# Sorting expert rows by one-hot products on TensorE in place of a trip through DRAM

## What is computed

```python
def _bank_residual(x2, Wr, br, W1, b1, W2, b2):     # twice: bank sp, bank fq
    logits = x2 @ Wr + br
    probs = softmax(logits); expert = argmax(probs); gate = probs[expert]
    oneh = one_hot(expert, 8)
    pos = (cumsum(oneh, axis=0) * oneh).sum(-1) - 1          # place within its expert
    slot = expert * CAP + pos                                # CAP is never reached here
    buf = zeros(...).at[slot].add(x2)                        # rows sorted by expert
    h = gelu(einsum('ecd,edf->ecf', buf, W1) + b1)           # 512 -> 128
    out = einsum('ecf,efd->ecd', h, W2) + b2                 # 128 -> 512
    return out.reshape(...)[slot] * gate                     # back to node order
# x = x + bank_sp + bank_fq + gelu(x2 @ Ws1 + bs1) @ Ws2 + bs2
```

## Time and profile before

| | us |
|---|---|
| median of 3 runs (522.31 to 524.74) | 523.99 |
| the profiled execution | 524.64 |
| its span, first to last instruction | 522.6 |
| TensorE busy in it | 468.2 (90%) |
| VectorE, ScalarE, GpSimd busy | 226.3, 180.3, 199.7 |

### The profile page before, as it was taken

One profiled execution on the slowest core, in us unless ns is written; L12 is line 12 of the kernel. 1 busy time (PEld: TensorE's weight loads), 2 busy tenths in 40 slices (PEclk: granted clock), 3 DMA queues, 4 the chain that ended last, 5 costly groups with the idle time before them and its releaser, 6 DMA issues.

```text
span 522.6 us, 7439 instructions
## 1 busy us (share of the span) xinstructions
PE 468.2 (90%) x2586; PEld 336.7 (64%) x2586; DVE 226.3 (43%) x559; ACT 180.3 (35%) x388; POOL 199.7 (38%) x217
## 2 busy tenths in 40 slices
PE   2788999989999997989999999999999999999930
PEld 2444547777665654766577777777777787887720
DVE  4879961313442727532220023320037665565542
ACT  2799672222211114511150033230265434333210
POOL 3103000191500802692507806142054847943422
PEclk9999899989999999999999999999999999999875
DMA  5999999968999789768207100304042532534665
GB/s 125 410 425 419 424 411 362 327 242 274 418 409 424 238 291 422 299 229 266 97 1 229 52 0 1 105 0 126 1 101 61 153 90 81 186 120 147 191 228 179
DMA packets 39636, 111.88 MB, mean 214 GB/s; under 512 B 6711, under 2 KB 12966, under 8 KB 31150
## 3 DMA queue, kind: packets, MB, share of 16 engines
q1 hardware_dynamic: 36558, 108.16, 56.8%
q0 software_dynamic: 3040, 3.22, 2.4%
HBM read 97.37 MB, written 13.98 MB: 213 GB/s over the span
## 4 chain that ended last, share of the span: by engine, by line
PE 74%; DMA 9%; issue 7%; POOL 3%; ACT 2%; SPq 2%; DVE 1%; POOLq 0%; DVEq 0%
PE ps L1457 16%; PE ps L1459 15%; PE ps L1458 15%; PE ps L1816 9%; PE ps L1481 8%; DMA ring<-in_L_gnn_basis_dram 8%; PE ps L1542 2%; POOL got L716 2%; PE ps L1661 2%; DMA got<-y_dram,slot_u 1%; ACT h_tmp L1217 1%; PE ps L1465 1%; POOL piece_lo L643 1%; PE ps L1719 1%; POOL piece_hi L642 1%
## 5 line engine op out<-in xcount | busy, mean ns | idle before, releaser
L1481 PE MATMUL ps<-ring,sel_att 128*32 128x512 f32 x512 | 66.1, 602 | 6.9 <-DMA ring<-in_L_gnn_basis_dram 3.4
L1457 PE MATMUL ps<-piece_hi,ht_hi 128*125 128x512 f32 x140 | 56.1, 401 | 0.8 <-PE ps L1459 0.6
L642 POOL CAST piece_hi<-piece_raw 128x512 fp32r<-128x512 f32 x28 | 19.8, 708 | 94.4 <-issue 69.9
L970 DVE SCALAR_TENSOR_TENSOR u_lo<-ps,gates,u_hi 125x512 fp32r<-125x512 f32 x20 | 15.0, 751 | 94.1 <-ACT u_hi L1365 94.1
L1458 PE MATMUL ps<-piece_lo,ht_hi 128*125 128x512 f32 x140 | 55.1, 394 | 0.0
L1459 PE MATMUL ps<-piece_hi,ht_lo 128*125 128x512 f32 x140 | 55.1, 394 | 0.0
L699 POOL TENSOR_TENSOR w_lo<-unit_raw,w_hi 128x512 fp32r<-128x512 f32 x32 | 40.5, 1291 | 33.2 <-ACT w_hi L1347 33.1
L643 POOL TENSOR_TENSOR piece_lo<-piece_raw,piece_hi 128x512 fp32r<-128x512 f32 x28 | 37.8, 1349 | 13.2 <-issue 11.1
L820 DVE TENSOR_SCALAR oh_n<-iota_n,keys 125x626 f16<-125x626 f16 x100 | 38.3, 383 | 8.0 <-PE ps L1542 5.9
L1816 PE MATMUL ps<-u_hi,cf 125*125 125x512 f32 x100 | 39.9, 399 | 1.3 <-PE ps L1459 1.3
L1816 PE MATMUL ps<-u_lo,cf 125*125 125x512 f32 x100 | 39.4, 394 | 0.0
(11 more groups left out here) (321 smaller groups left out, 982.7 us busy)
## 6 DMA issues: line engine op xcount, KB each, us to landing
ring<-in_L_gnn_basis_dram SPq DMA_DIRECT2D x64, 1024.0 KB, 9.3
y_dram<-ybuf SPq DMA_DIRECT2D x24, 256.0 KB, 2.0
rel_dram<-stag SPq DMA_DIRECT2D x16, 256.0 KB, 8.3
w_raw<-rel_dram SPq DMA_DIRECT2D x8, 512.0 KB, 7.0
unit_raw<-in_L_ffn_W_sp_dram SPq DMA_DIRECT2D x16, 256.0 KB, 3.0
unit_raw<-in_L_ffn_W_fq_dram SPq DMA_DIRECT2D x16, 256.0 KB, 2.8
piece_raw<-in_L_mix_Wkqv_dram SPq DMA_DIRECT2D x3, 1024.0 KB, 9.8
piece_raw<-in_L_mix_W_dram SPq DMA_DIRECT2D x2, 1024.0 KB, 10.2
```

The lines of the kernel that those rows point to most:

```text
L642: own_step(pool.tensor_copy(hi, raw))
L970: dve.scalar_tensor_tensor(out=u_lo[l][:, t, :], in0=ps[0:TP, u_bank(i), :], scalar=gates[:, t, r:r + 1], in1=u_hi[l][:, t, :].bitcast(F32 ...
L1457: pe.matmul(target, a_hi, b_hi, start=first, stop=False, skip_group_check=skip)
L1481: last = pe.matmul(ps[32 * c:32 * c + 32, rel_bank(ch), :], sel_att[:, ch // CHUNKS, g].rearrange("p r q -> p (r q)"), ring[slot][:, c * D ...
```

## The change

Slots come in blocks of 32 (`SB`): `NB` is 27 blocks a bank, 864 slots, taken four to a tile of up to 128 slots (`NY` = 7 tiles a bank, the last of three blocks). The way through DRAM (`scatter`, `read_back`, `turn_block_rows`, the zeroing) is gone. Instead GpSimd builds for each node tile a one-hot matrix of 125 rows x 864 slots (`sort_tile`), in three buffers in turn, and TensorE multiplies the rows with it (`sort_rows`), high part and rest, summed over five tiles in PSUM banks 2 and 1; ScalarE and VectorE copy out `sorted_h`, already turned. The second layer is done in full fp32 (`block_tile`): each block a product of 128 x 32 slots with 512 columns of W2, four beside one another in the partitions of one PSUM bank. W2 is no longer resident and split: SP loads to a register the expert's number of each block and fetches that expert's W2 for it (`load_w2`), to one of seven places (`HOME`), five of them used more than once and then after the product of the tile before (`o_mm`). The block tiles of bank fq come before the second half of the shared expert and the `e` tiles. The bias products are split over four places (`bias_sums`).

```diff
-NB = (NODES + E * 127) // 128
-SLOTS_OUT = NB * 128
+SB = 32
+NB = (NODES + E * (SB - 1)) // SB
+SLOTS_OUT = NB * SB
+NY = -(-NB // 4)
+P_TURNS = 3
...
+        HOME = [0, 1, 2, 3, 0, 1, 2, 4, 5, 3, 0, 1, 2, 6]
...
-        UNITS = ([(1, 0, e) for e in range(E)] + [(2, 0, e) for e in range(E)] + [(1, 1, e) for e in range(4)] +
-                 [(1, 2, 0)] + [(2, 1, e) for e in range(3)] + [(2, 2, 0)] + [(1, 1, e) for e in range(4, E)] +
-                 [(2, 1, e) for e in range(3, E)])
+        UNITS = ([(1, 0, e) for e in range(E)] + [(1, 1, e) for e in range(4)] + [(1, 2, 0), (2, 2, 0)] +
+                 [(1, 1, e) for e in range(4, E)])
...
             for n in range(RAWS, len(UNITS)):
-                if n == UNIT[2, 1, 4]:
-                    read_back(0)
                 load_unit(n)
-            for j in range(NB):
-                store_block(j)
-            read_back(1)
-            for j in range(NB, 2 * NB):
+            sp.wait_ge(rel_applied, 4)
+            sp.wait_ge(slots_ready, 2)
+
+            def load_w2(j):
+
+                if HOME[j] in HOME[0:j]:
+                    sp.wait_ge(o_mm, max(i for i in range(j) if HOME[i] == HOME[j]) + 1)
+                elif HOME[j] in (4, 5):
+                    sp.wait_ge(h_mm, 3 * NT)
+                b, i = divmod(j, NY)
+                for c in range(y_rows(j) // SB):
+                    at = b * NB + 4 * i + c
+                    expert = sp.value_load(block_ei[0:1, at:at + 1], min_val=0, max_val=E - 1)
+                    sp.dma_start(w2_home[HOME[j]][:, c, :], w2_of[b][bass.ds(expert, 1), :, :].rearrange("e f n -> f (e n)")
+                                 ).then_inc(w2_in[HOME[j]], 16)
+            for j in (0, 1, 2, 3, 2 * NY - 1):
+                load_w2(j)
+            for j in range(2 * NY):
+                if j < 3:
+                    load_w2(j + 4)
+                elif j == 3:
+                    for i in range(NY, NY + 3):
+                        load_w2(i)
+                elif j < NY:
+                    load_w2(j + 6)
                 store_block(j)
...
+            def sort_tile(b, t):
+
+                i = b * NT + t
+                if i >= P_TURNS:
+                    pool.wait_ge(sort_used, i - P_TURNS + 1)
+                pool.tensor_scalar(sort[:, i % P_TURNS, :], iota_s[:], slot_s[:, t, b:b + 1], None, ALU.is_equal).then_inc(sort_ready, 1)
...
+            for t in range(P_TURNS, NT):
+                sort_tile(0, t)
+                unit_rest(UNIT[1, 2, 0] + t - P_TURNS, UNIT[1, 2, 0] + t - P_TURNS + 1)
+            unit_rest(UNIT[1, 1, 4], len(UNITS))
+            for t in range(NT):
+                sort_tile(1, t)
             gather(0)
             gather(1)
...
+            def rest_of_rows(b, t):
+
+                dve.wait_ge(hidden_ready, 2 * (b * NT + t + 1))
+                if b:
+                    dve.wait_ge(sort_used, t + 1)
+                dve.scalar_tensor_tensor(out=rows_lo[:, t, :], in0=picked[b][:, t, :], scalar=gate_p[:, t, b:b + 1],
+                                         in1=rows_hi[:, t, :].bitcast(F32), op0=ALU.mult, op1=ALU.subtract).then_inc(lo_ready, 1)
...
+            dve.wait_ge(got_sp, 16 * NT)
+            for t in range(NT):
+                dve.tensor_tensor(x1[:, t, :], x1[:, t, :], got[0][:, t, :], ALU.add).then_inc(dve_own, 1)
+                n[0] += 1
+            dve.wait_ge(dve_own, n[0])
             for t in range(NT):
                 dve.wait_ge(ffn_mm, t + 1)
                 dve.tensor_tensor(x1[:, t, :], ps[0:TP, turn_bank("e", t), :], x1[:, t, :], ALU.add).then_inc(h_used, 1)
...
+            def sort_rows(b, t):
...
+                for rows in (rows_hi, rows_lo):
+                    for bank, a, z in SORT_BANKS:
+                        last = pe.matmul(ps[:, bank, 0:z - a], rows[:, t, :], sort[:, i, a:z],
...
+            def block_tile(j):
...
+                for c in range(y_rows(j) // SB):
+                    n = 4 * i + c
+                    last = pe.matmul(ps[c * SB:(c + 1) * SB, turn_bank("o", j), :], sorted_h[b][:, n * SB:(n + 1) * SB],
+                                     home[:, c, :], start=True, stop=True)
+                last.then_inc(o_mm, 1)
...
+            bias_sums(0, range(NT - 1))
+            for m in range(6, 4 * NT):
                 hidden(m)
+                if m % (2 * NT) == 2 * NT - 1:
+                    bias_sums(m // (2 * NT), [NT - 1])
+                j, i = m - 2 * NT - 2, m - NT - 2
+                if 0 <= i < NT:
+                    sort_rows(0, i)
+                if 0 <= i - 2 * NT:
+                    sort_rows(1, i - 2 * NT)
+                if m == 2 * NT + 2:
+                    bias_sums(1, range(NT - 1))
+                if 0 <= j < NY:
+                    block_tile(j)
+            shared(0, 0, 2)
+            sort_rows(1, 3)
+            shared(0, 2, KT)
+            sort_rows(1, 4)
+            for j in range(NY, 2 * NY):
+                block_tile(j)
+            shared(1, 0, KT)
```

More of the change, by code:

```diff
@@ L255, in gnn_mix_ffn @@
-        w2_lo = [place(f"w2_lo{b}", [128, E, D], F32R, a + 16384) for b, a in enumerate((r_h1t, r_ring))]
+        o = r_h1t
+        sort = place("sort", [TP, P_TURNS, SLOTS_OUT], F32R, o)
+        sorted_h = [place(f"sorted_h{b}", [128, SLOTS_OUT], F32, o + (P_TURNS + b) * SLOTS_OUT * 4) for b in range(2)]
+        o += (P_TURNS + 2) * SLOTS_OUT * 4
+        ybuf = [place(f"ybuf{b}", [128, NY, D], F32, a) for b, a in enumerate((o, r_split + 16384))]
+        o += NY * D * 4
+        w2_last = place("w2_last", [128, 3, D], F32, o)
@@ L259, in gnn_mix_ffn @@
[L259 to L266, removed]
+        ws2_hi = place("ws2_hi", [128, D], F32R, r_raw + RAWS * 2048)
@@ L518, in load_unit @@
                 if layer == 2:
-                    a = Ws2 if b == 2 else w2_of[b][e]
+                    a = Ws2
                 else:
@@ L1450, in _ @@
+            for j in range(8, 2 * NY, 2):
                 take_block(j)
+            shared_row(1)
         @block.tensor
@@ new lines, in bias_sums @@
+            def bias_sums(b, tiles):
+                if tiles[0]:
+                    pe.wait_ge(*bank_free("c", b))
+                elif b:
+                    pe.wait_ge(picked_ready, NT)
+                for t in tiles:
+                    for w in (b1_hi, b1_lo):
+                        last = pe.matmul(bias_sum(b, t), hot_t[:, t * TP:(t + 1) * TP], w[:, b, :], start=(t == tiles[0] and w is b1_hi),
+                                         stop=(w is b1_lo), skip_group_check=True)
+                last.then_inc(route_mm, 1)
@@ L1920, in block @@
+            def block_tile(j):
+                b, i = divmod(j, NY)
                 if i == 0:
-                    pe.wait_ge(unit_lo, UNIT[2, b, E - 1] + 1)
+                    pe.wait_ge(sorted_ready, 2 * b + 2)
+                home = w2_home[HOME[j]]
+                loads = sum(y_rows(n) // SB for n in range(j + 1) if HOME[n] == HOME[j])
+                pe.wait_ge(w2_in[HOME[j]], W2_SEEN[HOME[j]] + 16 * loads)
                 pe.wait_ge(*bank_free("o", j))
-                w_hi, w_lo = (a[b][:, bass.ds(expert_of[j], 1), :].rearrange("p e n -> p (e n)") for a in (w2_hi, w2_lo))
@@ L1924, in block, with shared @@
-                mm3(ps[:, turn_bank("o", j), :], back_hi[:, i, :], back_lo[:, i, :], w_hi, w_lo, True, True).then_inc(o_mm, 1)
+                for c in range(y_rows(j) // SB):
[3 more added lines that the diff above has]
+                last.then_inc(o_mm, 1)
+            def shared(h, a, b):
+                if a == 0 and h == 0:
+                    pe.wait_ge(unit_lo, UNIT[1, 2, 0] + 1)
+                    pe.wait_ge(picked_ready, 2 * NT - 1)
+                elif a == 0:
+                    pe.wait_ge(sorted_ready, 4)
+                for k in range(a, b):
+                    last = mm3(ps[:, h, 0:HALF], ws1_hi[:, k, :], ws1_lo[:, k, :], x1t_hi[:, k, h * HALF:(h + 1) * HALF],
+                               x1t_lo[:, k, h * HALF:(h + 1) * HALF], k == 0, k == KT - 1)
+                if b == KT:
+                    last.then_inc(h_mm, 1)
@@ L1957, in _ @@
             pe.wait_ge(route_t_ready, 1)
-            pe.wait_ge(slots_ready, 1)
-            for t, b in [(t, b) for b in range(2) for t in range(4)] + [(4, 0), (4, 1)]:
-                bank, c = ((0, 2)[b], t) if t < 4 else (1, b)
-                for w in (b1_hi, b1_lo):
-                    last = pe.matmul(ps[0:TP, bank, c * FF:(c + 1) * FF], hot_t[:, t * TP:(t + 1) * TP], w[:, b, :],
-                                     start=(c == 0 and w is b1_hi), stop=(w is b1_lo), skip_group_check=True)
```

265 lines of the change are left out of this document (109 added, 156 removed).

## The result

The changed kernel takes 535.65 us (median of 4 runs, 533.73 to 538.39) against 524.37 of the kernel before on the same chip (4 runs): ratio 1.0225, 95% interval 1.0165 to 1.0284. It is slower, by 1.7 to 2.8%. The forecast was 529.5 with a range of 512 to 539. The profiled execution took 538.39 us for a span of 536.6; it is the longest of the four, 2.7 us above the median.

What follows compares the result with a forecast made beforehand. SP's queue of W2 loads was to bound the changed kernel: 436.2 + 61.0 + 2.2 = 499.4, `gather(0)` 502.5, `gather(1)` 510.1, plus 17.5 and 0.5 gives 528.1, + 2.0 - 0.65 = 529.5 us; range 512 to 539.

Steps and rivals of the forecast that it cites:

- the signs of being wrong: SP's pitch under 1.0 us, SP idle waiting for `o_mm`, or `gather(0)` done before the last `y` store.
- SP's pitch: SyncE's queue: register load, address and issue take 1.13 us per W2 block, for 54 blocks.
- SP's start: SyncE's W2 loads start at 436 (435 to 438), after the first sort, GpSimd's compare and the rest of Ws1.
- nearer the cast: GpSimd's compare over 864 columns, no trace row: 1.0 us by the cast, 2.1 by the subtraction, 1.6 taken.
- Behind the last load: Store 6 to `gather(0)` 3.1 us, at 502.5; five gathers 7.6 us, so `gather(1)` begins at 510.1.
- The longer wait: Store 6, queued behind all W2 loads, holds the gathers longer than the last block tile, ending at 503, does.
- The tail: First fq gather to end of span: 17.5 us, left alone by the change, plus 0.5 for ten gathers in line.
- just inside: VectorE's ten adds of 0.69 us behind `gather(0)`'s landing at about 515 end at 521.9, in time.
- TensorE's cover: If only TensorE counted, the last block tile would end at 483.8, 17 us before today's 500.9.
- 8 in 1.06 us: TensorE's basis-sum row, from which a tile of four fp32 products was priced at 0.43 us, 0.45 taken.
- TensorE-bound, 507: Rival: with SP below 0.75 us a block, TensorE's 483.8 takes over, gather at 488, time 507; chance 0.08.
- Bytes: W2 transfers: 256 KB in 1.13 us is 232 GB/s, under 266 GB/s reached, so not the limit.

Runs made afterwards that it cites:

- the bulk kernel: Changed kernel with one SP register load bringing the expert numbers of all four blocks of a tile, run-time assertion removed: 520.65 us, ratio to before 0.9933.
- the store first: Changed kernel with only SP's order altered, a tile's y store ahead of the W2 loads of the tile six on: 538.51 us.
- the doubling: Kernel with one register load for four blocks and stores ahead of loads, the four block products of each tile issued twice: 529.33 us, against 522.15 without.
- the best form tried: Changed kernel with one register load for four blocks, first-bank y stores on ScalarE's queue and GpSimd's earlier start for SP: 519.90 us, ratio to before 0.9917.
- half the bytes: Changed kernel with each W2 load bringing 64 of the 128 rows and block products over 64 rows: 544.22 us.
- the fixed address: Changed kernel with each W2 load reading a fixed expert's matrix, no register load or address work: 520.11 us, ratio to before 0.9951.

## Why the prediction was right, and where not

The time lies in the range and the forecast's mechanism came: SP's register work paces the W2 loads, the last block tiles and store 6 wait for them, TensorE idles at a lower granted clock, and none of the signs of being wrong was seen. The median is 6.2 us over the forecast, and some terms were wrong without showing.

*SP's pitch, the main term*: 1.13 taken, 1.13 measured in the mean; the sum of parts from TensorE's queue carried over to SP's. The loads and six stores took 505.98 - 441.13 = 64.9 us for the 63.2 of the sum: a store among the loads cost some 0.6 us in the mean (1.6 to 2.0 us from the load before it to the load behind it) and was taken at 0.37. The Trainium skill, "DMA: Bandwidth & Descriptors", section "Latency and other measured facts", has some 600 ns as the floor of a register load; the row has 0.268 for one number, and the figure of the Trainium skill is passed only by the load of four (median 0.77 to 0.86). The same line of the Trainium skill says that the compiler unrolls four times by default to spread that cost; the bulk kernel spreads it another way, with one load for four numbers, and that was worth 15 us.

*SP's start*: 436.2 predicted, 441.1 seen. In part this is where the profiled execution stood: its first bias product is at 428.02, for 425.13 in the earlier trace rows. In the profiles of the edited kernels, with the same work ahead of it, it lies between 424.60 and 428.24. So most of these 2.9 us can be scatter of an execution; that the change has no part in them is not shown, as the kernel before has one profile only. The other 2.0 are a sum of small ones. The terms of the prediction (432.4 + 1.6 + 1.25) give 435.3 and not 436.2; without this slip, which helped, 2.9 us were missing. Of these 1.6 is the first four sorting products, done 8.9 us behind the first bias product and not 7.3 (0.94 of it an idle time of TensorE just before it), 0.4 a load of a W1 unit that SP still has to issue (440.70), and 0.85 the compare on GpSimd:

```profile
420.98 7.32 POOL L732 TENSOR_SCALAR sort<-iota_s,slot_s 125x864 fp32r<-125x864 f32 x3 [10.88 <-DVE slot_s L1121]
...
436.95 2.45 POOL L732 TENSOR_SCALAR sort<-iota_s,slot_s 125x864 fp32r<-125x864 f32 x1 [1.37 <-PE ps L1941]
```

A sort tile takes 2.44 us. I took 1.6 "nearer the cast" and gave 2.1 as the upper bound, by the subtraction of two inputs; a compare with a value per partition is dearer per element than either (2.44 / 864 = 2.8 ns against 1.25 / 512 = 2.4). This term was mis-sized, and its bound was no bound.

*Behind the last load*: store 6 to `gather(0)` took 3.9 us for 3.1, from `gather(0)` to `gather(1)` 8.6 for 7.6 (gather(1) was released by tile 13's store, not by its queue). Against the forecast of 529.5 the run's 535.65 is 6.2 more: 2.0 start, 1.7 loads, 0.8 and 1.0 here make 5.5. The tail held (536.6 - 518.49 = 18.1 us for 18.0), so the 0.7 left is in where the single executions stood against their medians.

*The longer wait*: a tie, taken for a clear case. "Another wait is longer", store 6 behind all loads, is on the chain of the profiled execution, but the other path was as long: tile 13's store released `gather(1)` 0.77 us after `gather(0)` was done, and taking store 6 out of the way brought nothing. The last block tile, which I had end at 503, ended at 512.7: the loads were out at 505.98 and not 499.4, and at the fallen clock a tile of four took 1.93 in place of 1.06. The landing of its store took 5 us instead of 3.1.

*VectorE*: "just inside" was on the path in this execution: adds without a gap from 522.63 to 532, with the last fq rows there at least 0.4 us before their add. So the chain went from store 6 over `gather(0)` and VectorE to the end, and not over `gather(1)` as forecast, and the two were tied again. With the store first the last adds waited for their rows as in the kernel before.

*TensorE's cover* (the time that its own work needs): wrong by 10 us, without harm to the forecast, since SP hid it; that is luck. From the first bias product to the end of the last block tile it takes 493.4 - 424.9 = 68.5 us where the prediction had 58.7. I read "8 in 1.06 us" in the earlier trace rows as eight products; it is four, as the doubling showed. A tile costs 0.86 us in a row and 1.00 between hidden tiles (452.19 to 453.19), 13.1 in all for 6.3; and a hidden tile behind one takes 2.97 (453.19 to 456.16) for 2.78, which would be the other 2.7 over 14 tiles; only seven stand behind a block tile, so part of it is unaccounted for. The change then does not take 5 us of work off TensorE but adds 1.5 (19.5 out, 7.9 + 13.1 in). The Trainium skill, "FP8 and Floating Point Precision", section "TensorE Precision Notes", with its four passes for true FP32, was right where I argued it away by my reading of the row: 0.86 us is four times 512 columns at 2.4 GHz. So the rival "TensorE-bound, 507" was really 518 to 522, which is what every kernel with SP out of the way and no product doubled gave; the best form tried is worth 4 us and not 17.

*Bytes*: rightly dismissed at a pitch of 1.1 us, and half the bytes show it. The reason given, 266 GB/s as what the stage reaches, was too low: 362 GB/s flowed.

## What to carry to other kernels

A load whose address comes from a register costs its queue the register load, the check, the address and the issue each time, here 1.13 us where the bare issue is 0.34: count these turns on the queue, and load many numbers with one instruction before changing anything else. Before a row is used as a price, count how many records one instruction leaves, by a second place where the number of instructions is known from the code. A price without its own row needs a bound from an instruction of the same kind, with the same operands, or a wide one. If two waits end together, removing one of them shows nothing.

## What was not expected of the hardware

A DMA issue over 64 partitions took 0.477 us and one over 128 partitions 0.338, with half the bytes. One register load of four numbers took 0.30 to 1.63 us (median 0.86) among outstanding transfers, more than three loads of one number at 0.27. Stores of 256 KB landed between 2.0 and 6.4 us after their issue on the bulk kernel. Both ends are in its last seven, 0.86 us apart: the first four landed in 2.0 to 2.8 us, the last in 6.4, with the first gathers issued from 490.46 on. On the same kernel the granted clock fell to 0.74 from 492 to 505 with TensorE busy all of the 13 us, and from 498 to 504 products of 512 columns show 0.62 us instead of 0.39; with the fixed address the same products had the full clock. What made the one fall and the other not was not found. It need not be the kernel: the ten executions of the bulk kernel have mean granted clocks from 0.976 to 0.990, the eight with the fixed address from 0.980 to 0.989.
